# Down projection of a gated layer: from plain products to seven Strassen products over output halves and row tiles

## What is computed

```
gate = lora_add(einsum('bnh,fh->bnf', x, W_gate), x, A_gate, B_gate)
up   = lora_add(einsum('bnh,fh->bnf', x, W_up), x, A_up, B_up)
act  = silu(gate) * up
down = lora_add(einsum('bnf,hf->bnh', act, W_down), act, A_down, B_down)
x = x + down
```

## Time and profile before

| | us |
|---|---|
| median of 3 runs | 2155.53 |
| lowest, highest | 2154.31, 2156.25 |
| profiled execution, device time | 2159.61 |
| profiled execution, span of the records | 2158.0 |
| mean granted TensorE clock | 0.994 |

### The profile page before, as it was taken

How to read it: one execution, slowest core, us unless ns; L and a number is a source line. 1 busy time by engine, 2 the same in 40 slices (tenths; PEclk the granted TensorE clock), 3 DMA queues, 4 the chain that set the end, 5 groups by cost and what they waited for, 6 DMA issues and landing times.

```text
span 2158.0 us, 34284 instructions
## 1 busy us (share of the span) xinstructions
PE 2085.9 (97%) x10432; PEld 1770.7 (82%) x10432; DVE 1611.2 (75%) x2134; ACT 967.1 (45%) x1269; POOL 111.9 (5%) x197
## 2 busy tenths in 40 slices
PE   2998999999999999999999999999999999999998
PEld 2998888878887788888888888888888888888887
DVE  7795999989998887878877337458887888753433
ACT  2222888778886433434343225333434333333222
POOL 3100000000001223200000000000000000000000
PEclk9999999999999999999999999999999999999999
DMA  5998999989998567743433986534343434255554
GB/s 167 340 338 331 338 352 352 345 319 344 360 360 301 160 178 195 204 106 97 109 97 107 282 235 214 185 106 128 97 109 97 109 92 109 70 152 189 195 176 135
DMA packets 260518, 441.53 MB, mean 205 GB/s; under 512 B 147638, under 2 KB 151926, under 8 KB 240758
## 3 DMA queue, kind: packets, MB, share of 16 engines
q1 hardware_dynamic: 246934, 410.79, 58.0%
q0 software_dynamic: 11360, 29.92, 4.6%
q10 hardware_dynamic: 2176, 0.26, 0.1%
HBM read 400.74 MB, written 63.73 MB: 215 GB/s over the span
## 4 chain that ended last, share of the span: by engine, by line
PE 85%; DVE 7%; DMA 3%; issue 2%; ACT 1%; DVEq 0%; SPq 0%; ACTq 0%
PE ps L2049 20%; PE ps L2050 19%; PE ps L2051 19%; PE ps L1971 5%; PE ps L1972 5%; PE ps L1973 5%; PE ps L1943 4%; DMA W<-in_w 2%; PE ps L2128 2%; PE ps L2127 2%; PE ps L1980 1%; DMA kept_rows<-X 1%; DVE part L1414 1%; PE ps L2164 1%; PE ps L2163 1%
## 5 line engine op out<-in xcount | busy, mean ns | idle before, releaser
L2049 PE MATMUL ps<-rows,oph 128*128 128x512 f32 x1196 | 468.3, 392 | 4.6 <-ACT tmp L867 4.0
L2050 PE MATMUL ps<-rows,oph 128*128 128x512 f32 x1196 | 467.8, 391 | 0.0
L2051 PE MATMUL ps<-rows,opl 128*128 128x512 f32 x1196 | 466.2, 390 | 0.0
L1414 DVE TENSOR_TENSOR part<-W,part 128x2048 fp32r<-128x2048 f32 x152 | 344.6, 2287 | 23.3 <-ACT part L802 22.9
L802 ACT ACTIVATE part<-W 128x2048 fp32r<-128x2048 f32 x152 | 291.0, 1917 | 105.8 <-DMA W<-in_w 99.0
L1510 DVE TENSOR_TENSOR tmp<-ps,tmp 128x512 f32<-128x512 f32 (+1 forms) x340 | 234.1, 689 | 129.3 <-PE ps L2128 65.1
L1507 DVE TENSOR_TENSOR wdl<-wraw,wdh 128x1024 fp32r<-128x1024 f32 x92 | 112.7, 1225 | 259.6 <-ACT wdh L867 259.6
L2049 PE MATMUL ps<-acb_h,wdh 128*128 128x512 f32 (+1 forms) x736 | 280.6, 381 | 2.5 <-DVE acb_l L1507 2.5
L2050 PE MATMUL ps<-acb_l,wdh 128*128 128x512 f32 (+1 forms) x736 | 279.6, 380 | 0.0
L2051 PE MATMUL ps<-acb_h,wdl 128*128 128x512 f32 (+1 forms) x736 | 279.6, 380 | 0.0
L2049 PEld LDWEIGHTS ps<-rows,oph 128*128 128x128 f32 x1196 | 225.6, 189 | 49.5 <-DVE opl L1507 4.5
(11 more groups left out here) (227 smaller groups left out, 2838.9 us busy)
## 6 DMA issues: line engine op xcount, KB each, us to landing
W<-in_w SPq DMA_DIRECT2D x152, 1024.0 KB, 7.2
raw<-in_wgu SPq DMA_DIRECT2D x168, 256.0 KB, 2.8
wraw<-in_wd SPq DMA_DIRECT2D x84, 512.0 KB
toep<-kpad SPq DMA_DIRECT2D x32, 1024.0 KB, 9.8
lraw<-picked_b SPq DMA_DIRECT2D x88, 256.0 KB, 4.1
raw<-kept_acts SPq DMA_DIRECT2D x88, 256.0 KB, 3.5
kept_acts<-tmp SPq DMA_DIRECT2D x84, 256.0 KB, 2.4
rraw<-kept_rows SPq DMA_DIRECT2D x36, 256.0 KB, 5.4
```

Source lines behind the costliest of these rows:

```text
L1414: V.tensor_tensor(out=wl[c][:], in0=W[:, c], in1=wh[c][:].bitcast(F32), op=ALU.subtract).then_inc(w_lo, 1)
L2049: mm(to, lhsT=wh, rhs=mh, start=start, stop=False)
L2050: mm(to, lhsT=wh, rhs=ml, start=False, stop=False)
L2051: return mm(to, lhsT=wl, rhs=mh, start=False, stop=stop)
```

## The change

The down projection of blocks 2 to 21 (20 blocks) is written as a product of 2x2 blocks: two halves of the output (512 of 1024) and, in the inner dimension, even and odd blocks of F; two row tiles on the other side. Strassen's scheme does it in seven products `d1` to `d7` instead of eight, with sums of sides and of rows. A panel now holds two blocks of F of one output half (128x1024, 512 KB in pieces of 2 KB) and two blocks of activations (128x1024, 512 KB). A product has five panels (`GROUPS`). The half block and block 1 are four plain quarters (`l11`, `l21`, `l12`, `l22`) with two panels each. There are 43 side panels and 39 row panels in a stage. The numbers `n` below count the side panels: `d1` 0 to 4, `d5` 5 to 9, `d6` 10 to 14, `d2` 15 to 19, `l11` 20 and 21, `d7` 22 to 26, `d4` 27 to 31, `l21` 32 and 33, `d3` 34 to 38, `l12` 39 and 40, `l22` 41 and 42.

The line numbers of the kernel after are others: its DVE helpers stand at L1609 and L1612 (L1507 and L1510 before).

```diff
+GROUPS = 5
+DOWN = ("d1", "d5", "d6", "d2", "l11", "d7", "d4", "l21", "d3", "l12", "l22")
...
+SUMMED_SIDE = ("d5", "d6", "d7", "d3")
+SUMMED_ROW = ("d5", "d6", "d7", "d4")
@@ SP
+            def load_side(st, n):
...
+                if n < 2:
                     sp.wait_ge(op_lo, (st + 1) * 7 * FT)
                 else:
+                    sp.wait_ge(side_lo, sides(st, n - 1))
...
+            def load_row(st, k):
...
+                    sp.wait_ge(row_lo, row_panels(st, k - 1))
...
+            def load_sums(st, g):
...
+                for n in range(2, NSIDE):
+                    if n == 3:
+                        store_acts(st, FT - 1)
+                    load_side(st, n)
+                    if n in ROW_END:
+                        load_row(st, ROW_END.index(n))
+                    if n < 2 + GROUPS:
+                        load_sums(st, n - 2)
+                    if n == 3:
+                        store_down_ranks(st)
+                    if n in (3, 4):
+                        for part in range(4):
+                            load_residual(2 * st + n - 3, part)
+                    if st == 0 and 5 <= n < 23:
+                        load_rows(1, 2 * (n - 5))
+                        load_rows(1, 2 * (n - 5) + 1)
+                    if st == 0 and n == 30:
                         sp.wait_ge(lora_next, SEQ * 4 * 16)
+                        sp.wait_ge(taken, 7)
                         load_projection(1, 0)
                         load_projection(1, 1)
@@ ACT
+            def cut_row_hi(st, k):
...
+                if k == 0:
+                    act.wait_ge(unit_step, at_step(st, FT - 1, P4))
...
+                else:
+                    act.wait_ge(panel_done, sides(st, ROW_END[k - 2] + 1))
+                copy(th[k % 2][:], src).then_inc(row_hi, 1)
@@ DVE
+            def panel_sums(st, n):
+
+                p, g = PANELS[n]
+                if p in SUMMED_SIDE:
+                    dve.wait_ge(side_in[n % 2], landed_in(st, n, NSIDE) * 32)
+                    new = wraw[:, n % 2]
...
+                if p in SUMMED_ROW:
+                    k = ROW_AT[p] + g
+                    dve.wait_ge(row_in[k % 2], landed_in(st, k, NROW) * 16)
...
+                for n in range(2, NSIDE):
+                    if n < NSIDE - 1:
+                        panel_sums(st, n + 1)
+                    panel_lo(st, n)
+                    take_product(st, n)
+                    if st == 0:
+                        new_rows_lo(n)
                 if st == 0:
                     half_unit_lo(1)
-                for o in range(LT):
-                    add_tile(o, 2 * st + 1)
+                take_last(st)
                 if st == 0:
+                    operand_lo(T4, rraw[LO[T4]][:], 20)
@@ PE
+            def product(st, p, start, stop, other=None):
+
+                for g in range(GROUPS):
+                    n, k = SIDE_AT[p] + g, ROW_AT[p] + g
+                    cut_panel(st, n, k)
+                    for pair in range(2):
+                        for o in range(4):
+                            last = side_by_rows(p, n, k, pair, o, start and g == 0 and pair == 0,
+                                                stop and g == GROUPS - 1 and pair == 1)
+                    last.then_inc(panel_done, 1)
...
-    nc = bacc.Bacc("TRN2", target_bir_lowering=False, num_devices=1)
+    nc = bacc.Bacc("TRN2", target_bir_lowering=False, num_devices=1, dynamic_dma_scratch_size=8192)
```

More of the change, by code:

```diff
@@ L333, in build @@
         t4_raw = sem("t4_raw")
-        bop_in = sem("bop_in")
+        bop_in = [sem(f"bop_in{k}") for k in range(3)]
         bop_hi = sem("bop_hi")
@@ new lines, in panel_lo, with take @@
+            def panel_lo(st, n):
+                cut_side_lo(st, n)
+                p, g = PANELS[n]
+                if g < ROWS_OF[p]:
+                    cut_row_lo(st, ROW_AT[p] + g)
+            def take(st, p, half, j, blocks=range(4)):
+                o0, n = blocks[0], len(blocks)
+                base = BANKS[p] + o0
+                rows = resid[j][:, :, 4 * half + o0:4 * half + o0 + n]
+                add(rows, ps[:, base:base + n].rearrange("p o (b h) -> p b o h", h=H), rows).then_inc(taken, 1)
@@ L2213, in unit @@
                 add_ranks(BANK_F, 0, 1, True).then_inc(unit_step, 1)
-            def down(tile, m, a, outs, start=False, stop=False, cols=slice(0, TILE)):
-                for o in outs:
-                    block = slice(o * P, (o + 1) * P)
-                    last = three(ps[:, o, cols], wdh[:, m % 2, block], wdl[:, m % 2, block],
-                                 acb_h[:, a, cols], acb_l[:, a, cols], start, stop)
-                    if stop and o < LT - 1:
-                        last.then_inc(tile_done, 1)
-                return last
@@ new lines, in cut_panel @@
+            def cut_panel(st, n, k):
+                pe.wait_ge(side_lo, sides(st, n + 1))
+                pe.wait_ge(row_lo, row_panels(st, k + 1))
+            def product(st, p, start, stop, other=None):
[3 more added lines that the diff above has]
+                    for pair in range(2):
+                        for o in range(4):
+                            last = side_by_rows(p, n, k, pair, o, start and g == 0 and pair == 0,
+                                                stop and g == GROUPS - 1 and pair == 1)
+                    last.then_inc(panel_done, 1)
+                    if g == 0 and other:
+                        other()
@@ new lines, in quarter @@
+            def quarter(st, p, start):
+                n, k = SIDE_AT[p], ROW_AT[p]
+                cut_panel(st, n, k)
+                for g in range(2):
+                    cols = slice(g * GC, (g + 1) * GC)
+                    for o in range(4):
+                        block = slice(g * TILE + o * P, g * TILE + (o + 1) * P)
+                        last = three(ps[:, BANKS[p] + o, cols], wdh[:, n % 2, block], wdl[:, n % 2, block],
+                                     th[k % 2][:, cols], tl[k % 2][:, cols], start and g == 0, False)
+                last.then_inc(panel_done, 1)
+                pe.wait_ge(side_lo, sides(st, n + 2))
+                for o in range(4):
+                    block = slice(o * P, (o + 1) * P)
+                    last = three(bank(BANKS[p] + o), wdh[:, (n + 1) % 2, block], wdl[:, (n + 1) % 2, block],
+                                 th[k % 2][:, TILE:2 * TILE], tl[k % 2][:, TILE:2 * TILE], False, True)
+                    if p == "l22" and o < 3:
+                        last.then_inc(block_done, 1)
+                last.then_inc(panel_done, 1)
```

587 lines of the change are left out of this document (324 added, 263 removed).

## The result

The changed kernel takes **2271.75 us** (median of 4 runs, 2270.9 to 2275.03) against 2154.92 of the kernel before on the same chip (2151.31 to 2156.25): a ratio of 1.0548, 95% interval 1.0536 to 1.0561. The forecast was slower, 2240 with a range of 2195 to 2285: the sign, the mechanism and the range hold, and the size was 32 us short. The profiled execution took 2272.14, its span is 2270.5.

A forecast was written before the change was run, and what follows sets the result against it. PE, busy for 97% of the span, was taken to bound the kernel. Per stage, 30.2 us saved and stalls added came to +29.9; twice, plus 20 and 4, gave +84 us: 2240, range 2195 to 2285.

The forecast's parts named there:

- the signs named: In the down stages: PE idle 60 to 85 us each, side cuts 7.2 us apart, one wait of about 15 us.
- The turn of 7.2 us: Summed products' loop: issue 0.1, row landing 3.6, three DVE operations 3.5, against PE's 5.44; 1.76 us of stall a turn.
- The Trainium skill's estimate of 4.1: Landing of 512 KB from the skill's figures; the turn would be 7.7 us and the time 2260.
- The two chains: Stalls per stage: +15.8 us for the cuts of n = 5 to 13, +20.3 for the sums of 22 to 31.
- the +4.6 put on them: Stage 0, row loads in 256-byte pieces together with the sums' loads at n = 5 and 6: +4.6 us in all.
- `d3` at 5.8: d3 sums only sides: five turns of 5.8 us, 29 us against PE's 24.5, so +4.5 a stage.
- The start, 15.5: Start of each stage: 14 queued transfers of 512 KB delay panel 4 to 39.7 us, PE being done at 24.2: +15.5.
- Stage 0 alone, +20: Extra cost in stage 0 from row loads in pieces, a late second chain and projection loads: 4.6, 7 and 8 us.
- The +7 for a second chain that begins late: Stage 0, n = 15 to 20: DVE has some 29 us of work, unevenly spread, so the second chain starts late: +7 us.
- Between the stages, +4: Stage 0 to 1: a 2.3 us T4 cut and four last takes stand ahead of the group 1 cut: +4 us.
- Scratch and takes at nothing: The halved descriptor scratch costs nothing; takes of 2.2 us each run while DVE waits for a landing, else 29 us a stage.
- The clock rival: PE's clock falls through the stalls, slowing panels to 10.9 us in part of the turns: 2290 us, chance 0.07.

The follow-up runs named there:

- the half side: The changed kernel with the side load of the summed sides (d5, d6, d7, d3) halved to 256 KB: 2251.1 us, ratio 1.0471.
- spread loads: The changed kernel with a stage's eight residual loads issued one a panel at n = 3 to 10, not four at 3 and four at 4: 2260.6 us.
- the order alone: The changed kernel with one line moved on DVE, the low cuts of panel n ahead of the sums of panel n + 1: 2168.49 us, ratio 1.0071.
- the stalls mended: The changed kernel with low cuts before sums, residual loads one a panel, and projection loads, row loads, takes and cuts reordered: 2139.16 us, ratio 0.9937.

## Why the prediction was right, and where it was short

- **What bounds it.** Right: the turn with a landing in it, ended by the row's low part on DVE, is what the trace shows, and moving one line, and the turn that follows the size of a load, prove it. Of the signs named, PE's idle time (60 to 85 us a stage) came out at 65 and 58, the turns at 8 to 9 instead of 7.2, and the long wait at 14.
- **The turn of 7.2 us.** This is the step that was mis-sized. Its three operations were right (1.15, 1.13, 1.22), the landing was not: 4.4 measured, 3.6 taken, which gives 7.9. The reason given, "the side's data are nearly through by then", was wrong, as the half side shows (3.8). The shortest row of an array with less ahead of it was the wrong neighbour; the middle between it and the median of 5.2 would have been nearer. The Trainium skill's estimate of 4.1 (DMA: Bandwidth & Descriptors, Latency and other measured facts) came nearer to the 4.4 of this trace, and so did the time that it gave, 2260.
- **What each part lost.** PE's starts give the time that each part of a stage took beyond PE's own pace (5.44 us a panel, 2.7 for a panel of a quarter), in us:

| part | forecast (stage 0, 1) | stage 0 | stage 1 |
|---|---|---|---|
| first start to panel 4 | 17.5, 17.5 | 16.7 | 16.9 |
| panel 4 to 13 (`d5`, `d6`) | 20.4, 15.8 | 29.0 | 23.3 |
| panel 13 to the second of `l11` | 7, 0 | 5.5 | 2.8 |
| from there to panel 30 (`d7`, `d4`) | 28.3, 20.3 | 30.2 | 25.6 |
| panel 30 to the last start | 6.5, 6.5 | 14 | 11 |

- **The two chains.** In stage 1 the eight turns after `d5`'s first panel have a mean of 8.04 and eight in `d7` and `d4` one of 7.96, where 7.2 was forecast. The first chain misses by 7.5. The second misses by 5.3 only because of a slip: ten turns and nine panels of PE were counted, where nine turns and eight panels lie; counted so, the forecast's own numbers give 18.6 and not 20.3, and the miss is 7.0. The turn's length is thus 14.5 of the 18.8 us by which stage 1 missed. In stage 0 `d5` and `d6` have 8.4 to 9.0 at a landing of 5.1: the +4.6 put on them should have been about 13, which is 8.6 of the 14.3 there.
- **`d3` at 5.8.** Five turns take 29.7 us in stage 1 and 30.3 in stage 0, against 29: right. But from panel 30 to the end PE lost 11 and 14 us where 6.5 was put down; the rest of this was not followed up.
- **The start, 15.5.** The wait was 14.0 and 14.1. The size is right, its cause only half: the queue is 8 of the 14 (spread loads: 5.6 left), yet the order alone cut it as well, since the wait needs both the late load and a sum that stands ahead of panel 4's cut.
- **Stage 0 alone, +20.** The projection's loads were put at 8: 6.2 at the wait, 2 to 8 in the time. The +7 for a second chain that begins late is no cost of stage 0 alone: PE waits 5.3 us ahead of `d7` in stage 0 and 5.1 in stage 1, and between the chains it loses 5.5 and 2.8. The loads in pieces: under 5 by the runs.
- **Between the stages, +4.** PE waits 4.5; the whole stretch is 6.3 longer. The other 2 were not followed up.
- **Before the stages, 0.** The first stage began 6.7 us earlier in this trace than in that of before. This is scatter: in the trace of the kernel before with the smaller scratch it began at 1162.9, 9.5 us earlier than in the first, and took the same 242.8. With this the misses add up: 14.3 + 18.8 + 2.3 - 6.7 is 29, the difference between 2243 and 2272.
- **Scratch and takes at nothing.** Right for both in the changed kernel, where the one turn with two takes (7.94) is no longer than its neighbours. The takes' cover goes once the landing is out of the turn: with the low cuts first a turn has 4.62 us without a take and 6.75 with one.
- **The clock rival.** The signal named (a clock under 0.97) came out at 0.970, so it deserves rows. Windows of the changed kernel (us, busy of PE, PEld, DVE, ACT, POOL; clock, DMA share, GB/s), and ACT around the second:

```profile
1194.00:1207.00 13.00, 2.82 (x7) 2.27 (x8) 5.17 (x5) 2.11 (x2) 0.00 (x0) 0.50 1.03 330
...
2153.00:2156.40 3.40, 3.40 (x10) 2.66 (x9) 1.84 (x2) 0.00 (x0) 0.00 (x0) 0.50 0.42 154
```

```profile
2149.33 1.06 ACT L938 ACTIVATE wdh<-wraw 128x1024 fp32r<-128x1024 f32 x1 [4.22 <-PE ps L2238]
...
2158.91 1.06 ACT L938 ACTIVATE wdh<-wraw 128x1024 fp32r<-128x1024 f32 x1 [7.58 <-PE ps L2238]
```

The clock did fall to its lower level, 1.2 GHz, with the 14 us wait and again after short ones: here PE had waited 2.24 us, until 2151.47. From 2153.0 to 2156.4 PE had it, and ACT took the next high part at 2158.91, which is 9.6 us after the one before and so 1.6 late. DVE needs that part here,

```profile
2165.30 1.22 DVE L1609 TENSOR_TENSOR wdl<-wraw,wdh 128x1024 fp32r<-128x1024 f32 x1
```

5 us after ACT has it. So a slow panel turns waiting into busy time, and the turn (2148.98 to 2156.93, 7.95) stays as long as the one before it (7.93), in which PE has the full clock: here the clock followed the stalls and did not set the time. No run holds the clock apart from the stalls, so for the other turns this is argued from these two and from the landings that end DVE's waits in them. With the stalls mended it is back at 0.992 (0.994 before).

## What to carry to other kernels

An engine's busy time of 4.6 us in 5.44 says only that the work could fit; write down one turn of the loop and see whether a load's landing stands between two operations of that engine. If the engine frees a buffer and then waits for what is loaded into it, put its independent work in between: here one moved line was worth over 100 us, which is more than the 240 matmuls that the change takes away. And take a landing's price from a row with the same traffic just ahead of it on the queue, not from the shortest row of that size.

## What the runs showed of the hardware that I had not expected

- 512 KB of one queue lands in 4.4 us when 512 KB were issued 1.1 us ahead of it, in 3.8 behind 256 KB, and 256 KB behind 512 in 3.4.
- SP itself can be held for long by an issue. Early in stage 0 of the changed kernel a pair of row loads in pieces of 256 bytes takes 7.98 us to issue, and a later pair 1.39:

```profile
1191.74 7.98 SPq L654 DMA_DIRECT2D rraw<-kept_rows  x2
...
1212.86 1.39 SPq L654 DMA_DIRECT2D rraw<-kept_rows  x2
```

Both the queue and the pieces have a part in it: with the same bytes read in whole rows the first pair takes 3.13, and with the residual loads spread 6.08. Here it costs nothing, since the next load waits for DVE's cut until 1202.93 in any case.
